# Where TensorE's operands begin: fillers of 352 and 480 bytes, and a row of Wv of 1152 columns

## The reference

```python
h = layernorm(x) * (1 + ca) + sa
q, k, v = h @ Wq.T, h @ Wk.T, h @ Wv.T            # 1024 columns each, 16 heads of 64
log_decay = -softplus(h @ Wd.T + bd)              # 16 columns
k = k * sigmoid(h @ Wg.T)
s_t = exp(log_decay_t) * s_{t-1} + k_t^T v_t      # per head, over the tokens
o_t = q_t s_t
o = rmsnorm(o) * norm_w * sigmoid(h @ Wog.T)
x = x + ga * (o @ Wo.T)
h = layernorm(x) * (1 + cb) + sb
xr, xk = mixes of h with the token before it
x = x + gb * sigmoid(xr @ W_r) * (relu(xk @ W_k)**2 @ W_v)
```

## The kernel before

| product | moving columns | offset |
|---|---|---|
| g, q, k projections | 256 | 192 |
| scores | 256 | 0 |
| k2 | 256 | 64 |
| v, blocks 0 to 3 | 264 | varies with the row |
| v, blocks 4 and 5 | 512 | varies with the row |
| og, o | 512 | 0 |
| r, v2 | 512 | 448 |

## Time and profile before

### The profile page before, as it was taken

One profiled execution on the slowest core, in us unless ns is written; L12 is line 12 of the kernel. 1 busy time (PEld: TensorE's weight loads), 2 busy tenths in 40 slices (PEclk: granted clock), 3 DMA queues, 4 the chain that ended last, 5 costly groups with the idle time before them and its releaser, 6 DMA issues. The chain is left out here.

```text
span 3672.8 us, 73725 instructions
## 1 busy us (share of the span) xinstructions
PE 3596.5 (98%) x25349; PEld 3339.3 (91%) x25349; DVE 2145.5 (58%) x5207; ACT 1546.0 (42%) x3904; POOL 464.7 (13%) x883
## 2 busy tenths in 40 slices
PE   7999999999999999999999997899999999999998
PEld 7999999999999999999999997688888888888887
DVE  4555555555555555555555556566566655666566
ACT  4445445445545445445445453333332323233332
POOL 0111111111111111111111111100000000000000
PEclk8999999999999999999999999899999999999999
DMA  4222322322322322322232223412221122212220
GB/s 156 76 60 65 81 60 58 87 62 56 87 63 55 86 64 54 81 71 54 75 77 54 75 71 87 162 69 71 77 91 69 69 80 85 75 69 74 75 91 23
DMA packets 206044, 274.89 MB, mean 75 GB/s; under 512 B 13968, under 2 KB 146080, under 8 KB 206000
## 3 DMA queue, kind: packets, MB, share of 16 engines
q1 hardware_dynamic: 206000, 274.31, 25.6%
HBM read 189.84 MB, written 84.41 MB: 75 GB/s over the span
## 5 line engine op out<-in xcount | busy, mean ns | idle before, releaser
L813 POOL TENSOR_TENSOR k_lo<-kg,k_hi 128x256 fp32r<-128x256 f32 x256 | 186.7, 729 | 1501.1 <-ACT q_hi L588 1501.1
L609 ACT ACTIVATE decay<-cum_rows,w_cur 128x128 f32<-128x128 f32 x1024 | 327.8, 391 | 20.6 <-POOL cum_rows L807 12.7
L55 PE MATMUL psJ<-h_hi,w_g_hi 128*128 128x256 f32 x1024 | 314.7, 307 | 8.3 <-DVE h_lo L675 4.6
L577 ACT COPY q<-psJ 128x256 f32<-128x256 f32 x256 | 95.5, 373 | 501.1 <-PE psJ L57 501.1
L55 PE MATMUL psJ<-h_hi,w_q_hi 128*128 128x256 f32 x1024 | 304.4, 297 | 0.0
L683 DVE SCALAR_TENSOR_TENSOR kg<-gate,psJ 128x256 f32<-128x256 f32 x256 | 107.8, 421 | 333.0 <-PE psJ L57 305.5
L56 PE MATMUL psJ<-h_lo,w_q_hi 128*128 128x256 f32 x1024 | 286.2, 279 | 0.0
L57 PE MATMUL psJ<-h_hi,w_k_lo 128*128 128x256 f32 x1024 | 286.1, 279 | 0.0
L56 PE MATMUL psJ<-h_lo,w_g_hi 128*128 128x256 f32 x1024 | 285.9, 279 | 0.0
L57 PE MATMUL psJ<-h_hi,w_q_lo 128*128 128x256 f32 x1024 | 285.8, 279 | 0.0
L55 PE MATMUL psJ<-h_hi,w_k_hi 128*128 128x256 f32 x1024 | 285.6, 279 | 0.0
(11 more groups left out here) (226 smaller groups left out, 10601.8 us busy)
## 6 DMA issues: line engine op xcount, KB each, us to landing
cum_rows<-cum_dram SPq DMA_DIRECT2D x256, 256.0 KB, 5.4
o_rows_dram<-o SPq DMA_DIRECT2D x256, 128.0 KB, 1.8
o_rows<-o_rows_dram SPq DMA_DIRECT2D x32, 1024.0 KB, 5.4
an_norm_x<-in_L_attn_x_dram SPq DMA_DIRECT2D x32, 512.0 KB, 3.9
h_dram<-h_hi SPq DMA_DIRECT2D x32, 512.0 KB, 2.7
h_dram<-h_lo SPq DMA_DIRECT2D x32, 512.0 KB, 3.8
h_hi<-h_dram SPq DMA_DIRECT2D x32, 512.0 KB, 3.7
h_lo<-h_dram SPq DMA_DIRECT2D x32, 512.0 KB, 4.6
```

The costliest lines, as they stand in the source:

```text
L55: nc.tensor.matmul(out, w_hi, x_hi, start=first, stop=False)
L577: nc.scalar.copy(q[:, b, :], psJ[USES.index(("q", b)) % 2][:, 0:T]).then_inc(s["by_act"], 1)
L609: last = nc.scalar.activation(decay[:, 2 * c + h, :], cum_rows[:, p % 4, 2 * c + h, :], ACT.Exp, bias=w_cur[:, 3, c, 2 * p + h:2 * p + h + ...
L813: nc.gpsimd.tensor_tensor(k_lo[:, :], kg[:, p, :], k_hi[:, :].bitcast(F32), ALU.subtract).then_inc(s["k_lo"], 1)
```

## The change

`a_filler` grows from 8 to 88 columns (32 to 352 bytes), `b_filler` from 8 to 120 (32 to 480 bytes), and the tile of Wv from 1040 to 1152 columns (rows of 4608 bytes, 9 x 512; the last 112 columns hold nothing). The four blocks of v of 264 columns become blocks of 256 and 272, so that each begins at a multiple of 128 columns, and the second block of 512 begins at column 640 instead of 528. The total of columns is the same (528 + 512). In the code's arithmetic every large product of both passes then has offset 0: 160 + 352 = 512 bytes ahead of hT, and 32 + 480 = 512 ahead of mix.

```diff
-VZ = (512 + H) // 2
+V_PARTS = ((0, 256), (256, 256 + H), (640, 512))
...
-        sb("a_filler", [P, 8])
+        sb("a_filler", [P, 88])
...
-                    c, at, n = (b // 2, b % 2 * VZ, VZ) if b < 4 else (b - 4, 512 + H, 512)
+                    c = b // 2 if b < 4 else b - 4
+                    at, n = V_PARTS[b % 2 if b < 4 else 2]
...
-                last = nc.scalar.copy(v[:, b // 2, 0:VZ], bank[:, 0:VZ])
+                last = nc.scalar.copy(v[:, b // 2, 0:256], bank[:, 0:256])
             else:
-                nc.scalar.copy(v[:, b // 2, VZ:512], bank[:, 0:512 - VZ])
-                last = nc.scalar.copy(zt[:, 0, b // 2, :], bank[:, 512 - VZ:VZ])
+                nc.scalar.copy(v[:, b // 2, 256:512], bank[:, 0:256])
+                last = nc.scalar.copy(zt[:, 0, b // 2, :], bank[:, 256:256 + H])
...
-        sb("b_filler", [P, 8])
+        sb("b_filler", [P, 120])
...
-            W = {name: pair(first, name, KD, HID + H if name == "v" else HID) for name in "qgkv"}
+            W = {name: pair(first, name, KD, 1152 if name == "v" else HID) for name in "qgkv"}
...
-                    at = n * (512 + H) if name == "v" else n * 512
+                    at = n * V_PARTS[2][0] if name == "v" else n * 512
```

## The result

The median went from 3674.75 us (four runs, 3674.07 to 3676.39) to 3699.7 us (four runs, 3696.4 to 3701.05): ratio 1.0066, 95% interval 1.0053 to 1.0079. The forecast was 3700. The profiled execution took 3696.4 us, its span is 3694.7. Its distance to the profiled execution of before, 21.9 us of span, is thus 3 us smaller than that of the medians; it is the fastest of its four.

The account below looks back on a forecast made before the run. PE was taken as the bound, its time being products by spacing. Projections +32, k2 +3.5, r and v2 -9, v -1.5 and +0.5 sum to +25.5 us on 3674.6: 3700 us, range 3655 to 3709.

Parts of the forecast that it names:

- What bounds the kernel: Both passes: PE, busy 3596.5 of 3672.8 us; time is the number of its products by their spacing.
- Projections: First pass, g, q and k, offset 192 to 0: they settle near the scores' 120.0 ns, +32 us.
- rival C: 256-column products: place makes no difference, how a chain begins does; -15 us, 3660 us; chance 0.17.
- The terms of that product: Projections of g, q and k: 8704 steps times (119.6 - 115.9) ns, giving +32 us.
- k2: Second pass, k2 products, offset 64 to 0: 1536 spacings go from 117.7 to 120.0 ns, +3.5 us.
- r and v2: Second pass, offset 448 to 0: 1536 products go from 233.6 to o's 226.8 ns, taken as -9 us.
- v with 512 columns: First pass, 768 v products: 231 to 226.8 ns, -3.2 us if settled at once, taken as -1.5 us.
- v with 256 and 272: First pass, v blocks formerly 264 columns: 256 at 120.0 ns, 272 at 124; together +0.5 us.
- The sum: All terms of both passes together: +25.5 us on the profiled execution's 3674.6 us, so 3700 us.
- Rival B: 256-column products: offset 0 is best, all chains settle at 113.5 ns; -45 us, 3629 us; chance 0.15.
- rival D: Whole kernel: nothing comes of it, offsets don't set the spacing or gains and losses cancel; 3675 us; chance 0.12.
- z = 0.57: Share of 256-column steps at 120.0 ns, the rest at 113.5, where the sum is zero; below it the kernel is faster.

Follow-up runs that it names:

- a_only: Kernel before with a_filler alone grown from 8 to 88 columns, so g, q and k have offset 0: 3707.4 us against 3676.5, ratio 1.0082.
- after_v192: Changed kernel with 192 bytes more ahead of Wv, putting g, q and k back at offset 192: 3669.1 us against 3675.0 for the kernel before, ratio 0.9982.
- b_only: Kernel before with b_filler alone grown from 8 to 120 columns, so r, v2 and k2 have offset 0: 3670.5 us against 3676.5, ratio 0.9984.
- s256: Kernel before with a_filler of 24 and b_filler of 56 columns, offset 256 for g, q, k, k2, r and v2: 3700.6 us, executed once.
- x208_k64: Kernel before with h_hi and h_lo 16 bytes further (offset 208 for g, q, k), r and v2 at 0, k2 at 64: 3691.1 us, executed once.

## Why the prediction was right

- *What bounds the kernel.* PE's products alone moved the end: 21.4 us more of busy PE in 21.9 us more of span, no wait that grew by more than 1 us.
- *Projections, +32 us forecast, 31 to 32 measured.* The step that carried it was to take the six scores for the projections' stand-in and to read their equal steps as a state that holds. In the projections it does hold; a_only shows it without the rest of the change, after_v192 shows the opposite. But the reading of the scores was in part luck. Rows 7 are the cleanest of the 256 groups of six in the trace of before: only 31 groups, one in nearly every tile, have all their steps at 119 to 121 ns. Thirty groups have the steps of this one (in ns 202, 118, 125, 113, 119):

```profile
1092.06 0.36 PE L55 MATMUL psS<-q_hi,k_hi 128*128 128x256 f32 x1
1092.27 0.28 PE L56 MATMUL psS<-q_lo,k_hi 128*128 128x256 f32 x1
1092.38 0.29 PE L57 MATMUL psS<-q_hi,k_lo 128*128 128x256 f32 x1
1092.51 0.28 PE L55 MATMUL psS<-q_hi,k_hi 128*128 128x256 f32 x1
1092.62 0.28 PE L56 MATMUL psS<-q_lo,k_hi 128*128 128x256 f32 x1
1092.74 0.28 PE L57 MATMUL psS<-q_hi,k_lo 128*128 128x256 f32 x1
```

Of the scores' steps without a stop 56% were 119 to 121 ns, 31% were 116 to 118 and 5% were 113 or 114. So "the scores have neither", said against rival C, doesn't hold over all groups. That 120 ns is where a chain ends and not one of the steps that it passes through was seen only in the chains of the changed kernel.
- *The terms of that product.* The means came out as assumed, 115.9 to 119.6 ns over the steps of g, q and k together. The count didn't: 8141 steps are free of stops and not 8704: the chains of g and those of q both stand behind small fp32 products, and each loses about two steps to them, so that it is 4 in 36 and not 2. The 8141 steps give 30.6 us; the rest lies in the steps around the stops.
- *k2, +3.5 forecast, +3.0 measured; r and v2, -9 forecast, -9.6 measured.* 1.2 of the 9.6 is the half clock of the last tile's r, so the spacings gave -8.4. b_only repeats both terms alone: +3.0 and -9.1.
- *v with 512 columns, -1.5 forecast, -1.9 measured.* One of two blocks settles at once, the other doesn't; I had neither, only their middle.
- *v with 256 and 272, +0.5 forecast, +1.1 measured.* 272 columns cost 125.5 ns and not the 124 between my bounds.
- *The sum*, +25.5 forecast, is +24.7 by the starts (+25.9 without the clock's share) and +25.0 by the medians. The two profiled executions differ by 21.9 us only, and the four of the changed kernel span 4.6 us, so that 3699.7 lies within 1 us of the 3700 forecast is luck; that it lies within a few us is not.
- *Rival B* (113.5 ns at offset 0) is refuted: not one k product at 276 ns in the changed kernel, a_only or s256. *Rival C* (the place makes no difference to 256 columns) by the same runs, *rival D* by b_only and a_only, each of which is off the time of before beyond its interval, in opposite directions. The point z = 0.57 at which B turned into a loss left out v, which B's own 3629 us counts; with v it is a little over 0.6. The forecast doesn't rest on it.
- The rule of the Trainium skill, "TensorE: Matmul & The Clock Gate", section "Back-to-back issue gap", has the gap depend on columns and clock alone and gives 109 ns for 256 columns and 216 for 512. The section calls this the gap of a single product, and the prediction took it for chains; for a stream of loads and products, which these chains are, it states some 131 ns for 512 columns. The runs show means of 115.2 to 120.0 and of 226.7 to 234.0, moved by the operands' places at a granted clock of 1.00, and no chain of 512 columns below 226.6. Here the measurement decides.
- The number 512, modulo which the offsets are counted, rested on no row. The period is 256, so the change could have done with other fillers; for the forecast it made no difference, as 0 is 0 in both.

What stays open is why. Two reads of one memory that get in each other's way, the load for the next product and the moving operand of this one, would fit an effect of their distance with a period; no run here shows the memory itself, and the irregular values at 16 and 32 bytes were not explained. Nor was it tried what puts a chain at offset 192 into the one state or the other. The trace of before shows that it isn't chance: each tile has eight chains of k products, and over the 32 tiles the first, second and last of them have the 113.3 ns 29, 28 and 30 times, the fifth 14 times and each of the other four once. So something that recurs in each tile decides, such as what stands ahead of the chain.

## What to carry to other kernels

When PE is the bound, measure its spacing (distance of starts over a chain), rather than its durations or its busy share, and group it by shape and by the distance of the two operands' addresses: a filler of some hundred bytes between two tiles was worth -0.3% to +0.8% of the whole kernel. The good place differs by shape: here 0 for 512 moving columns, but for 256 it is 192 (g, q, k) or 32 (k2), and 0 is the worst or level with the worst; one rule for all large products gave away with the many what it won with the few. Before an edit moves operands, look for an operation in the trace that stands at the new place already: the scores' 120.0 ns, less 0.4 ns that I allowed for settling, priced 9216 projections to within 1 us. Then look at all its groups and not at one: what a chain of 24 settles to shows only in part in chains of six.

## What the runs showed of the hardware that I had not expected

- The spacing of these fp32r products depends on the distance of the two operands, as far as two pairs show with a period of 256 bytes: offsets 0 and 256 agree within 0.2 ns in g, q, k and k2 and within 0.4 in r and v2, 192 and 448 within 0.2 ns. For r and v2 only the first pair was run. 128 bytes are no period, and a moving operand 16 bytes further cost 3 ns (x208_k64).
- The settled values at the clock of 2.4 GHz are round: 113.3 ns is 272 cycles, 120.0 is 288, 226.7 is 544, that is 17, 18 and 17 cycles for 16 columns. No chain of large products in any run was faster than 17 for 16, to within 0.2%.
- A chain keeps the state that it falls into within a few products, and at one offset there can be two such states: of the 256 chains of k products in before, at offset 192, 105 have a mean of 113.3 ns and 151 one of 117.7, and none lies between; at others the k products' steps stay spread, over 115 to 122 ns at 128 and 160 and over 114 to 125 at 208.
